# Three weighted tiles summed by VectorE, folded once by TensorE behind the next slot's first tile

## The chip, the cores and the metric

The kernel runs on one core of a Trainium2 chip. The metric is the device time of one execution in microseconds (us), lower is better; a profiled execution gives the trace that is read here. The engines of the core that matter are TensorE (PE; its weight loads are listed as PEld), VectorE (DVE), ScalarE (ACT), GpSimd (POOL, which here issues gathers) and SyncE (SP, which here only issues DMAs).

## What is computed

The reference runs a batch of 16 images (32 channels, 64 by 64 pixels) through four residual blocks, each behind a group normalisation: a Winograd convolution, a deformable convolution, a small network of quantised convolutions, and a convolution with an edge branch and channel attention. The change lies in the second block:

```python
py = hs[None, None, :, None] + ky[None, :, None, None] + dy
px = ws[None, None, None, :] + kx[None, :, None, None] + dx
sampled = _bilinear_sample(x, py, px)          # [B, C, 9 taps, H, W]
s = sampled.reshape(B, GROUPS, cin_g, KK, H, W)
wg = w.reshape(GROUPS, cout_g, cin_g, KK)
y = jnp.einsum('bgikhw,goik->bgohw', s, wg).reshape(B, Cout, H, W)
```

## The kernel before

**Images and slots.** The four blocks of three neighbouring images are interleaved. One image's work is a period of 24 slots (SLOTS), each of three steps q = 0, 1, 2. In period n every engine walks through the same slots: the deformable sampling of image n, then what stands in `c(n - 1, s, q)` (the last two blocks of the image before), `a(n + 1, s, q)` (the first block, the offsets and the tables of the next image) and `first(n + 2, s, q)`. Each engine's program is this list in order, written out by hand, with semaphores between the engines; an engine that waits holds up all that stands behind it. The periods 1 to 14 are one loop, which all engines leave and enter at its edge. A place is written (slot, step) below, as in the code.

**Two ways of sampling.** Of the nine taps, six (GTAPS) are gathered from a table in DRAM by GpSimd's indirect DMAs into `ring`, eight blocks deep, and VectorE weights the four corners of each sample (`weigh_corners`, line 1165), adds rows (`add_rows`, 1169) and adds columns (`add_columns`, 1175, which also frees the ring's block). The other three taps (DT) are sampled densely. A slot is one dense tap of one eighth of the image (a part; parts are g = s // 3, and e = s % 3 is the tap).

**A slot's dense work.** ScalarE makes `select`. TensorE makes three row tiles (`row_tile`, line 1445: three matmuls in the program, six in the trace, 128x512 out) into one of two banks of `ps_r`; tile t may start when tile t-2 has been weighed (`tile_weighed`). VectorE multiplies each with the hats of its columns (`weigh_tile`, line 1154), into `col_hat` itself, which is double buffered by slot and loaded by a DMA of SyncE (`load_cols`, line 460). At the end of a slot, behind its third tile and whatever stands at step 2, TensorE folds each of the three weighed tiles with four small matmuls (`fold_dense`, line 1457; 24 records a slot in the trace) into `ps_y`. In a part's last slot (e = 2) it also turns the gathered values (`turn`, line 1471) and folds them (`fold`, 1478), and ScalarE saves `ps_y` at the start of the next part (`save_conv`, 669).

**SyncE.** In a slot SyncE first issues the load of the next slot's `col_hat`, which waits until the slot before has been folded, and then the copies of the other blocks: `copy_taps` (line 410, twelve DMAs) behind the normalised images "norm1" (VectorE's place (12, 0)), "norm2" (3, 0) and "norm3" (19, 0), and `store_plane` and `load_taps` (416, 422) behind each "relu" (6, 1), (9, 2) and (12, 2). These bring the convolutions at TensorE's places (5, 2), (8, 2), (11, 2), (14, 1), (14, 2) and (21, 2) their input.

**Corner weights.** The weights of the gathered taps are computed for the next image at (22, 2) into `w_next` (line 1135), and copied to `w_cur` at (23, 0) (line 1210).

## Time and profile before

| | us |
|---|---|
| median of 3 runs | 4684.99 (4672.83 to 4689.32) |
| the profiled execution | 4687.73 |
| its span | 4685.9 |
| TensorE busy | 4264.4 (91%) |
| GpSimd busy | 3263.5 (70%) |
| VectorE busy | 2932.8 (63%) |
| ScalarE busy | 1812.5 (39%) |
| mean granted TensorE clock | 0.973 |

The busy time of an engine is the union of its instructions' times. It is an average over stages that have different limits: the same engine can have every microsecond taken in some slots and stand idle for 10 us in others. So the trace is also read by stretches of one period. A mean duration of an instruction is longer than the distance from its start to the next one's where instructions overlap in an engine's pipeline, which holds for TensorE above all.

### The profile page before, as it was taken

The numbers are of one execution on the slowest core, as the hardware profiler recorded it, in microseconds if no ns is written. First come the engines' busy times: TensorE is split into PE (matmuls) and PEld (weight loads), VectorE is DVE, ScalarE is ACT, GpSimd is POOL, SyncE is SP. The second block draws the span as 40 slices with busy tenths as digits, with TensorE's granted clock in tenths as the row PEclk, the third lists the DMA queues.
The fourth block names the chain that finished last, engine by engine and source line by source line (L and its number), as shares of the span: only waits on it lengthen the run. The fifth ranks groups of instructions, "written<-read, shape, count | busy, mean of one in ns | idle before, by whom it ended". The sixth has DMA issues, their size and how long they took to land.

```text
span 4685.9 us, 74289 instructions
## 1 busy us (share of the span) xinstructions
PE 4264.4 (91%) x24997; PEld 2037.6 (43%) x24997; DVE 2932.8 (63%) x5482; ACT 1812.5 (39%) x1991; POOL 3263.5 (70%) x3094
## 2 busy tenths in 40 slices
PE   2799999999999999999999999999999999999992
PEld 2344444444444444444444444444444444444440
DVE  4556666666656766666666656665666666656552
ACT  1343434344434433434344334434434344334331
POOL 1777777777777767777676777767777676767740
PEclk8899999999999999999999999999999999999995
DMA  4577877877878686777768777686777868778752
GB/s 104 197 232 214 240 232 221 236 223 227 235 222 240 208 245 215 231 235 224 237 215 240 222 222 230 212 244 209 237 230 220 237 214 243 219 218 244 219 185 66
DMA packets 479569, 1024.32 MB, mean 219 GB/s; under 512 B 261924, under 2 KB 298116, under 8 KB 474628
## 3 DMA queue, kind: packets, MB, share of 16 engines
q1 hardware_dynamic: 325636, 516.15, 38.7%
q10 hardware_dynamic: 55296, 302.01, 18.6%
q0 software_dynamic: 98304, 201.52, 15.5%
q8 instruction: 233, 3.82, 0.3%
q14 instruction: 100, 0.82, 0.1%
HBM read 864.66 MB, written 73.99 MB: 200 GB/s over the span
## 4 chain that ended last, share of the span: by engine, by line
PE 57%; DVE 16%; DMA 11%; SPq 9%; issue 6%; ACT 1%; ACTq 0%; POOL 0%; DVEq 0%; POOLq 0%
PE ps_r L1445 40%; SPq L410 6%; DMA col_hat<-coord_table 5%; PE ps_c L1431 4%; DVE col_hat L1154 4%; PE ps_y L1457 4%; DMA wino<-xn_a 3%; PE ps_a L1384 2%; DVE ring L1165 2%; PE ps_a L1431 2%; DMA taps_c<-plane_act 2%; PE ps_t L1471 1%; DVE ring L1169 1%; DVE values L1175 1%; PE ps_y L1478 1%
## 5 line engine op out<-in xcount | busy, mean ns | idle before, releaser
L593 POOL DMA_INDIRECT ring<-patch_table,idx_part x3072 | 3254.9, 1060 | 1258.8 <-issue 1049.5
L1445 PE MATMUL ps_r<-select,image 128*128 128x512 f32 x6912 | 3166.2, 606 | 73.9 <-issue 47.7
L1445 PEld LDWEIGHTS ps_r<-select,image 128*128 128x128 f32 x6912 | 1273.7, 192 | 1526.1 <-issue 1490.2
L1154 DVE TENSOR_TENSOR col_hat<-ps_r,col_hat 128x512 f32<-128x512 f32 x1152 | 793.4, 689 | 1530.1 <-PE ps_r L1445 1201.1
L643 ACT ACTIVATE select<-row_in,minus_row 128x1536 f32<-128x1536 f32 x384 | 605.0, 1575 | 765.3 <-PE ps_r L1445 698.5
L645 ACT ACTIVATE select<-select,one_col 128x1536 f32<-128x1536 f32 x384 | 605.3, 1576 | 12.5
L1165 DVE TENSOR_TENSOR ring<-ring,w_cur 128x768 f32<-128x768 f32 x512 | 487.2, 952 | 15.2 <-DMA ring<-patch_table,idx_part 13.2
L662 ACT COPY samples<-ps_t 128x512 f32<-128x512 f32 x256 | 149.6, 585 | 886.7 <-PE ps_t L1471 886.7
L1457 PE MATMUL ps_y<-col_hat,w_dense 128*32 128x128 f32 x9216 | 379.4, 279 | 100.8 <-DVE col_hat L1154 94.9
L1457 PEld LDWEIGHTS ps_y<-col_hat,w_dense 128*32 128x32 f32 x9216 | 215.8, 109 | 307.5 <-DVE col_hat L1154 160.7
L1169 DVE TENSOR_TENSOR ring<-ring 128x384 f32<-128x384 f32 x512 | 283.2, 553 | 4.4
L1175 DVE TENSOR_TENSOR values<-ring 128x192 f32<-128x192 f32 x512 | 181.6, 355 | 20.0
L1471 PEld LDWEIGHTS ps_t<-ident,values 128*128 128x128 f32 x1024 | 128.1, 141 | 135.6 <-issue 135.6
L1384 PEld LDWEIGHTS ps_a<-wino,w_freq 128*128 128x128 f32 x1152 | 141.9, 201 | 48.2 <-issue 26.1
L1384 PE MATMUL ps_a<-wino,w_freq 128*128 128x64 f32 x1152 | 142.5, 284 | 22.0 <-DVE wino L937 22.0
L1471 PE MATMUL ps_t<-ident,values 128*128 128x128 f32 x1024 | 153.9, 273 | 0.0
L669 ACT ACTIVATE conv_out<-ps_y,vec 128x128 f32<-128x128 f32 x128 | 46.7, 365 | 276.1 <-PE ps_y L1478 276.1
L710 ACT ACTIVATE work_c<-ps_c,bn_bias,bn_scale 128x512 f32<-128x512 f32 x160 | 116.7, 779 | 75.8 <-PE ps_c L1431 60.8
L678 ACT COPY wino<-ps_a 128x384 f32<-128x384 f32 x96 | 44.5, 479 | 251.5 <-PE ps_a L1384 245.1
L1431 PE MATMUL ps_a<-wino,w_off 96*32 96x512 f32 x768 | 96.4, 656 | 31.6 <-DMA wino<-xn_a 31.6
L1431 PE MATMUL ps_c<-taps_c,w_signs 96*32 96x512 bf16 x1152 | 75.7, 399 | 46.6 <-DMA taps_c<-plane_act 46.6
L1431 PE MATMUL ps_c<-taps_c,w_edge_conv 96*32 96x512 f32 x768 | 96.1, 636 | 12.4 <-DMA taps_c<-xn_c 12.4
(231 smaller groups left out, 2362.5 us busy)
## 6 DMA issues: line engine op xcount, KB each, us to landing
row_in<-coord_table ACTq DMA_DIRECT2D x384, 768.0 KB
col_hat<-coord_table SPq DMA_DIRECT2D x384, 768.0 KB
ring<-patch_table,idx_part POOLq DMA_INDIRECT x3072
taps_c<-plane_act SPq DMA_DIRECT2D x144, 268.1 KB
taps_c<-xn_c SPq DMA_DIRECT2D x192, 130.0 KB
coord_table<-wino SPq DMA_DIRECT2D x64, 216.0 KB
wino<-xn_a SPq DMA_DIRECT2D x96, 130.0 KB
plane_act<-act_c SPq DMA_DIRECT2D x192, 65.0 KB
```

The costliest lines, as they stand in the source:

```text
L410: sp.dma_start(dst[dx * C:(dx + 1) * C, lo - dx:hi - dx], src[s * C:(s + 1) * C, lo - s * RS * XW:hi - s * RS * XW]).then_inc(done, 16)
L593: nc.gpsimd.indirect_dma_start(out=ring[j][:, h % 2, k, :], out_offset=None, in_=table, in_offset=bass.IndirectOffsetOnAxis(ap=idx_part[:, ...
L643: nc.scalar.activation(sel, row_in[s % 2][:], ACT.Abs, bias=minus_row[:]).then_inc(row_in_read, 1)
L645: nc.scalar.activation(sel, sel, ACT.Relu, bias=one_col[:], scale=-1.0).then_inc(select_made, 1)
L1154: v.tensor_tensor(hat_t, ps_r[:, (s + t) % 2], hat_t, ALU.mult).then_inc(tile_weighed, 1)
L1165: return chain.add(v.tensor_tensor(tile, tile, wts, ALU.mult))
L1169: return chain.add(v.tensor_tensor(tile[:, :, 0:2 * C], tile[:, :, 0:2 * C], tile[:, :, 2 * C:], ALU.add))
L1384: ins = mm(ps_a[:, f % 2, b_ * NT:(b_ + 1) * NT], flat_w(w_freq, f * FREQ + b_), wino_v[:, f, :, b_, :], start=True, stop=True)
L1431: ins = mm(ps[s * C:(s + 1) * C, h], w[:, k0 + dy], src[:, r0:r0 + RS // 2, 0:W], start=(dy == 0), stop=(last and dy == 2))
L1445: ins = mm(ps_r[:, (s + t) % 2], image[:, m, t], select[s % 2][:, m], start=(m == 0), stop=(m == PAIRS - 1))
L1457: ins = mm(ps_y[j * C:(j + 1) * C, :], w_dense[:, DT - 1 - e].rearrange("p g o -> p (g o)"), col_hat[s % 2][:, t, j * P:(j + 1) * P], star ...
L1471: ins = nc.tensor.transpose(ps_t[:, j * P:(j + 1) * P], values[:, g % 2, j, 4 * k:4 * k + 4].rearrange("p k c -> p (k c)"), ident[:])
```

## The change

VectorE adds the three weighed tiles of a slot in two instructions (`sum_tiles`): tile 0 + tile 1 at step 1, and + tile 2 at step 2, both behind the gathered block's work of the step and ahead of the other blocks' work. The sum goes to a new double-buffered `tile_sum`. TensorE folds this sum alone, with four matmuls instead of twelve in the program, and does so one slot later, behind the next slot's first row tile (`fold_before`); the folds of the gathered values move with it. SyncE's load of `col_hat` now waits for the sums and no longer for the fold. ScalarE saves `ps_y` behind the next slot's `select` and no longer ahead of it. Two pieces of the other blocks swap their steps on VectorE in slot 0: `add_conv` goes from (0, 1) to (0, 2), and the first piece of `a` from (0, 2) to (0, 1). The corner weights are computed in place in `w_cur`, without the copy. The padded taps of `values` are gone: the second chunk of the turn reads taps 2 to 5 instead of 4 to 7, with zero weights for the two that the first chunk has had.

```diff
@@ SyncE, load_cols
                 if not known_zero(n) or s >= 2:
-                    sp.wait_ge(dense_folded, (n * SLOTS + s - 1) * WT)
+                    sp.wait_ge(tiles_summed, n * SLOTS + s - 1)
@@ ScalarE, slot
-                if e == 0 and live(before[0]):
-                    save_conv(*before)
                 if s != SLOTS - 2:
                     rows_ahead(n, s)
...
                 if e == 0 and live(n) and g < PARTS - 2:
                     place(n, g + 2)
+                if e == 0 and live(before[0]):
+                    save_conv(*before)
@@ VectorE, a and c
-                if at == (0, 2):
+                if at == (0, 1):
                     dve.wait_ge(halo_a, n * 32 + 32)
...
-                if at == (0, 1):
+                if at == (0, 2):
                     add_conv(n)
@@ VectorE, the corner weights at (22, 2)
+                    if not known_zero(n):
+                        dve.wait_ge(weighted, n * Q + RING)
...
-                        ins = v.tensor_tensor(w_next[:, :, :, i], hat[:, i // 2, 0, :, 0:GTAPS],
+                        ins = v.tensor_tensor(w_cur[:, :, :, i], hat[:, i // 2, 0, :, 0:GTAPS],
@@ VectorE, gathered_block
                             dve.wait_ge(a_dve.sem, a_dve.at(m, "weights"))
-                            if live(n):
-                                dve.wait_ge(weighted, m * Q + RING)
-                            chain.step(v.tensor_copy(w_cur[:], w_next[:]))
@@ VectorE, new
+            def sum_tiles(n, s, t):
+
+                to, hats = tile_sum[:, s % 2], col_hat[s % 2]
+                dve.wait_ge(tile_weighed, (n * SLOTS + s) * WT + t + 1)
+                if t == 1:
+                    if not known_zero(n) or s >= 2:
+                        dve.wait_ge(dense_folded, n * SLOTS + s - 1)
+                    tiles_added[0] = chain.add(v.tensor_tensor(to, hats[:, 0], hats[:, 1], ALU.add))
+                else:
+                    chain.upto(tiles_added[0])
+                    v.tensor_tensor(to, to, hats[:, 2], ALU.add).then_inc(tiles_summed, 1)
@@ VectorE, slot
                     gathered_block(n, s, q)
+                    if q > 0 and live(n):
+                        sum_tiles(n, s, q)
@@ TensorE, fold_dense
-                for t in range(WT):
-                    pe.wait_ge(tile_weighed, (n * SLOTS + s) * WT + t + 1)
-                    for j in range(JB):
-                        ins = mm(ps_y[j * C:(j + 1) * C, :],
-                                 w_dense[:, DT - 1 - e].rearrange("p g o -> p (g o)"),
-                                 col_hat[s % 2][:, t, j * P:(j + 1) * P], start=(e == 0 and t == 0), stop=False)
-                    ins.then_inc(dense_folded, 1)
+                pe.wait_ge(tiles_summed, n * SLOTS + s + 1)
+                for j in range(JB):
+                    ins = mm(ps_y[j * C:(j + 1) * C, :],
+                             w_dense[:, DT - 1 - e].rearrange("p g o -> p (g o)"),
+                             tile_sum[:, s % 2, j * P:(j + 1) * P], start=(e == 0), stop=False)
+                ins.then_inc(dense_folded, 1)
@@ TensorE, slot
                     if live(n):
                         row_tile(n, s, q)
+                    if q == 0:
+                        fold_before(n, s)
+                    if live(n):
                         if e == DT - 1 and q != 1:
                             turn(n, g, q // 2)
...
-                if live(n):
-                    fold_dense(n, s)
-                    if e == DT - 1:
-                        for k in range(CHUNKS):
-                            fold(n, g, k)
```

On TensorE, before, the first slot of the loop and the start of the second, with what each instruction waits for:

```order
414 L1445 MATMUL ps_r<-select,image 128x512 [waits tile_weighed]
415 L1445 MATMUL ps_r<-select,image 128x512 x2
417 L1445 MATMUL ps_r<-select,image 128x512 [waits tile_weighed,image_ready]
418 L1445 MATMUL ps_r<-select,image 128x512 x2
421 L1445 MATMUL ps_r<-select,image 128x512 [waits tile_weighed]
422 L1445 MATMUL ps_r<-select,image 128x512 x2
424 L1457 MATMUL ps_y<-col_hat,w_dense 32x128 [waits tile_weighed,conv_saved]
425 L1457 MATMUL ps_y<-col_hat,w_dense 32x128 x3
427 L1457 MATMUL ps_y<-col_hat,w_dense 32x128 [waits tile_weighed]
428 L1457 MATMUL ps_y<-col_hat,w_dense 32x128 x3
430 L1457 MATMUL ps_y<-col_hat,w_dense 32x128 [waits tile_weighed]
431 L1457 MATMUL ps_y<-col_hat,w_dense 32x128 x3
```

The same place in the changed kernel:

```order
312 L1469 MATMUL ps_r<-select,image 128x512 [waits tile_weighed]
313 L1469 MATMUL ps_r<-select,image 128x512 x2
315 L1480 MATMUL ps_y<-tile_sum,w_dense 32x128 [waits tiles_summed]
316 L1480 MATMUL ps_y<-tile_sum,w_dense 32x128 x3
318 L1501 MATMUL ps_y<-samples,w_dconv 32x128 [waits copied]
319 L1501 MATMUL ps_y<-samples,w_dconv 32x128 x3
321 L1501 MATMUL ps_y<-samples,w_dconv 32x128 [waits copied]
322 L1501 MATMUL ps_y<-samples,w_dconv 32x128 x3
324 L1469 MATMUL ps_r<-select,image 128x512 [waits tile_weighed,image_ready]
325 L1469 MATMUL ps_r<-select,image 128x512 x2
328 L1469 MATMUL ps_r<-select,image 128x512 [waits tile_weighed]
329 L1469 MATMUL ps_r<-select,image 128x512 x2
```

The three folds that waited for the slot's own weighed tiles are gone from its end. Behind the first tile stands one fold, of the slot before, and here, at a part's start, the folds of the gathered values too.

On VectorE, before, the second slot of the loop up to its third weighed tile:

```order
475 L1154 TENSOR_TENSOR col_hat<-ps_r,col_hat 128x512 [waits rows_made]
476 L1169 TENSOR_TENSOR ring<-ring 128x6x64 [waits dve_chain]
477 L893 BN_STATS bn_c<-x 128x6 [waits x2_ready]
478 L893 BN_STATS bn_c<-x 128x6
479 L895 BN_AGGR mv_c<-bn_c 128x2 [waits dve_chain]
481 L1154 TENSOR_TENSOR col_hat<-ps_r,col_hat 128x512 [waits rows_made]
482 L1175 TENSOR_TENSOR values<-ring 128x192 [waits turned,dve_chain]
483 L922 TENSOR_TENSOR wino<-xn_a 128x288
484 L923 SCALAR_TENSOR_TENSOR wino<-xn_a 128x288
485 L924 SCALAR_TENSOR_TENSOR wino<-xn_a 128x288
487 L1154 TENSOR_TENSOR col_hat<-ps_r,col_hat 128x512 [waits rows_made]
488 L1327 COPY x_cur<-x_next 128x1024 [waits x2_ready]
```

The same place in the changed kernel, from the second tile on:

```order
529 L1165 TENSOR_TENSOR col_hat<-ps_r,col_hat 128x512 [waits rows_made]
530 L1200 TENSOR_TENSOR values<-ring 128x192 [waits turned,dve_chain]
531 L1174 TENSOR_TENSOR tile_sum<-col_hat 128x512 [waits dense_folded,tile_weighed]
532 L930 TENSOR_TENSOR wino<-xn_a 128x288
533 L931 SCALAR_TENSOR_TENSOR wino<-xn_a 128x288
534 L932 SCALAR_TENSOR_TENSOR wino<-xn_a 128x288
536 L1165 TENSOR_TENSOR col_hat<-ps_r,col_hat 128x512 [waits rows_made]
537 L1177 TENSOR_TENSOR tile_sum<-tile_sum,col_hat 128x512 [waits dve_chain,tile_weighed]
538 L1351 COPY x_cur<-x_next 128x1024 [waits x2_ready]
```

Each of the two adds stands between the weighing of a tile and the other blocks' instructions, so all of these, and the weighing of the next tile, stand behind it.

## Rows read from the trace of the kernel before

**Rows 1.** The profile's page: busy times, and the chain that ended last by engine.

```profile
PE 4264.4 (91%) x24997; PEld 2037.6 (43%) x24997; DVE 2932.8 (63%) x5482; ACT 1812.5 (39%) x1991; POOL 3263.5 (70%) x3094
...
PE 57%; DVE 16%; DMA 11%; SPq 9%; issue 6%; ACT 1%; ACTq 0%; POOL 0%; DVEq 0%; POOLq 0%
```

**Rows 2.** Groups by line: busy us, mean ns, idle before them and its releasers.

```profile
L593 POOL DMA_INDIRECT ring<-patch_table,idx_part x3072 | 3254.9, 1060 | 1258.8 <-issue 1049.5 <-ACT idx_part L621 143.4 <-DVE values L1175 65.8
L1445 PE MATMUL ps_r<-select,image 128*128 128x512 f32 x6912 | 3166.2, 606 | 73.9 <-issue 47.7 <-DVE col_hat L1154 15.2 <-ACT image L654 10.8
...
L1154 DVE TENSOR_TENSOR col_hat<-ps_r,col_hat 128x512 f32<-128x512 f32 x1152 | 793.4, 689 | 1530.1 <-PE ps_r L1445 1201.1 <-DMA col_hat<-coord_table 325.2 <-issue 0.8
...
L1165 DVE TENSOR_TENSOR ring<-ring,w_cur 128x768 f32<-128x768 f32 x512 | 487.2, 952 | 15.2 <-DMA ring<-patch_table,idx_part 13.2
L1457 PE MATMUL ps_y<-col_hat,w_dense 128*32 128x128 f32 x9216 | 379.4, 279 | 100.8 <-DVE col_hat L1154 94.9 <-issue 2.3
L1169 DVE TENSOR_TENSOR ring<-ring 128x384 f32<-128x384 f32 x512 | 283.2, 553 | 4.4
...
L1210 DVE COPY w_cur<-w_next 128x768 f32<-128x768 f32 x16 | 10.3, 644 | 0.0
```

**Rows 3.** One period in nine windows: length, busy time by engine, clock, DMA share, GB/s.

```profile
2353.60:2382.60 29.00, 28.43 (x155) 13.56 (x154) 24.44 (x46) 11.11 (x11) 22.91 (x21) 1.00 0.48 171
2382.60:2405.90 23.30, 22.72 (x118) 11.81 (x116) 14.18 (x27) 9.17 (x9) 17.81 (x19) 1.00 1.01 294
2405.90:2444.20 38.30, 37.89 (x244) 19.58 (x243) 20.96 (x34) 14.79 (x17) 26.58 (x28) 1.00 0.60 185
2444.20:2466.40 22.20, 20.43 (x133) 9.74 (x132) 20.82 (x36) 11.76 (x14) 17.02 (x16) 1.00 0.57 195
2466.40:2489.50 23.10, 21.10 (x138) 10.25 (x137) 11.66 (x23) 6.81 (x9) 17.99 (x17) 1.00 0.79 222
2489.50:2516.60 27.10, 24.34 (x130) 10.06 (x132) 13.50 (x22) 9.52 (x8) 20.88 (x20) 1.00 0.98 259
2516.60:2578.50 61.90, 60.48 (x384) 29.36 (x377) 42.90 (x86) 27.05 (x31) 37.63 (x37) 1.00 0.82 240
2578.50:2606.70 28.20, 26.98 (x165) 11.57 (x164) 19.11 (x43) 9.23 (x12) 22.50 (x19) 1.00 0.79 211
2606.70:2632.90 26.20, 21.99 (x115) 10.27 (x115) 14.65 (x25) 13.34 (x16) 20.32 (x20) 0.87 0.91 287
```

**Rows 4.** TensorE's timeline at four places: start, duration, instructions, idle before them.

```profile
2324.36 0.86 PE L1457 MATMUL ps_y<-col_hat,w_dense 128*32 128x128 f32 x24
2325.15 5.42 PE L1445 MATMUL ps_r<-select,image 128*128 128x512 f32 x12
...
2344.36 0.62 PE L1478 MATMUL ps_y<-samples,w_dconv 128*32 128x128 f32 x16
2349.04 5.37 PE L1445 MATMUL ps_r<-select,image 128*128 128x512 f32 x8 [4.06 <-issue]
...
2505.38 0.42 PE L1457 MATMUL ps_y<-col_hat,w_dense 128*32 128x128 f32 x8 [0.21 <-issue]
2505.73 2.84 PE L1445 MATMUL ps_r<-select,image 128*128 128x512 f32 x6
```

**Rows 5.** Timelines of SyncE and VectorE around norm2, and of TensorE's waits for copies.

```profile
2385.36 8.71 SPq L410 DMA_DIRECT2D taps_c<-xn_c  x12
...
2405.86 0.69 DVE L1154 TENSOR_TENSOR col_hat<-ps_r,col_hat 128x512 f32<-128x512 f32 x1 [7.93 <-DMA col_hat<-coord_table]
...
2465.51 0.70 DVE L1224 TENSOR_SCALAR act_c<-work_c 128x1024 bf16<-128x1024 f32 x1
...
2484.06 1.50 PE L1431 MATMUL ps_c<-taps_c,w_signs 96*32 96x512 bf16 x24 [1.20 <-DMA taps_c<-plane_act]
...
2513.05 5.36 PE L1431 MATMUL ps_a<-wino,w_off 96*32 96x512 f32 x48 [1.46 <-DMA wino<-xn_a]
```

**Rows 6.** GpSimd's gathers by line while VectorE stood idle, 2398 to 2405.8 us.

```profile
L593 POOL DMA_INDIRECT ring<-patch_table,idx_part x7 | 6.6, 945 | 2.1 <-issue 2.1
```

29 lines of the change are left out of this document (22 added, 7 removed).

## The prediction

> **What bounds the kernel now.** I read the page first, then the groups by line, then one period cut into windows, then the timelines where a window shows an engine waiting. By its busy share TensorE is the bound: 4264.4 of 4685.9 us, against 2932.8 of VectorE [rows 1]. But the chain that ended last is only 57% TensorE; 16% of it is VectorE, 20% are DMAs and SyncE's issues [rows 1]. So the bound changes hands within a period, and one number for the kernel will not do. The windows show where [rows 3]. In slots 5 to 7, and 14 to 19, TensorE is busy for 37.89 of 38.30 and 60.48 of 61.90 us, and VectorE for little more than half or two thirds: TensorE's time. In slots 8 and 9 VectorE is busy for 20.82 of 22.20 us and TensorE for 20.43: VectorE's time. In slots 0 to 2 both are near full (28.43 and 24.44 of 29.00). The rest hangs on copies. The load of `col_hat` for slot 5 stands on SyncE behind the twelve copies that norm2 starts: 8.71 us of issues from 2385.36 on, and the tile is weighed only at 2405.86, after VectorE had stood for 7.93 us, 20.5 us behind norm2 whatever TensorE does meanwhile [rows 5]. The convolution at (11, 2) waited 1.20 us for its copy, which starts with the relu that ends at 2466.2, and the one at (14, 1) waited 1.46 us for a copy behind norm1 [rows 5].
>
> A third engine is close. A gather takes 1060 ns [rows 2] and about 0.30 us of issue follows it (2.1 us behind 7) [rows 6], so the 192 gathers of an image take 192 x 1.36 = 261 us. The period that I cut is 279.3 us (the sum of the nine windows) [rows 3]. GpSimd can shorten its waits by 18 us a period, no more.
>
> **What TensorE saves.** Today 24 small matmuls take 0.79 us from their start to the next tile's (2324.36 to 2325.15); 8 take 0.35 us (2505.38 to 2505.73) [rows 4]. That is 0.44 us a slot, 384 x 0.44 = 169 us. Ahead of the folds TensorE also waits for VectorE's last tile, 94.9 us in all [rows 2], 0.25 us a slot; behind the next slot's first tile (2.6 to 2.8 us) that wait is covered, if VectorE gets its weighing, a block's 0.95 and 0.55 us and the add done in this time. Together 264 us, 16.5 us a period, were TensorE the bound throughout.
>
> **What VectorE pays.** No instruction of before adds 128x512 from SBUF to SBUF. The 128x384 add takes 553 ns and the 128x768 product 952 ns [rows 2], so 128x512 lies between: 553 + 128 x (952 - 553) / 384 = 686 ns, and the weighing itself, of the same shape, takes 689 [rows 2]. Back to back such instructions overlap by some 0.04 us; I take 0.65 us of path for each, with 0.55 and 0.69 as the ends. Two a slot are 1.3 us, 31 us a period. The copy to `w_cur` that goes gives back 0.64 us a period [rows 2], in slot 23, where VectorE waits anyway: nothing. The waits of the adds for their own engine's results find them done, but for the drain. VectorE's busy time a period goes from 182 (the sum in rows 3) to 182 + 31 = 213 us: still under TensorE's, but not in every window.
>
> **By windows** [rows 3], change against before:
> - Slots 0 to 2. VectorE 24.44 + 3.9 = 28.3, and 0.5 us a slot that it idles even where it is the bound (slots 8 and 9: (22.20 - 20.82) / 2 = 0.7): 29.8 for 29.0, **+0.8**. TensorE's saving is lost here.
> - Slots 3 and 4. Norm2 to the weighing of slot 5 is a chain of issues and a DMA: **0**. The adds behind norm2 lie in VectorE's 7.93 us of idle time; without that cover they would cost 2.6.
> - Slots 5 to 7: three times 0.44 and some of the wait, **-1.5**.
> - Slots 8 to 11. VectorE 20.82 + 2.6 + 1.0 = 24.4 for 22.2 in the first two, +2.2, and with that the relu at the end of (9, 2), whose copy the convolution at (11, 2) awaits. In this period all of it would come through; TensorE's waits for such DMAs are not in all periods, so I take half, +1.1, and -0.5 for slot 11 behind the convolution: **+0.6**.
> - Slots 12 and 13. Norm1 stands ahead of the adds of its slot, the copies take what they take: **0**.
> - Slots 14 to 19. Six slots, 42.90 + 7.8 = 50.7 us of VectorE in 61.9: TensorE's. Six times 0.44 and part of 0.25: **-3.0**.
> - Slots 20 and 21. VectorE's edge values at (21, 2), which TensorE awaits, come behind one or two adds more, +1.3; the folds behind them are gone, -0.9: **+0.4**.
> - Slots 22 and 23: -0.5, and at the period's end 24 + 16 small matmuls (0.79 and 0.62 us less overlap) leave the path to the loop's edge, whose 4.06 us of issue stay [rows 4]; they return as 0.35 + 0.5 behind the first tile, in VectorE's time: -1.5. **-2.0**.
>
> The sum is -4.7 us a period, -66 over the 14 full ones; images 0 and 15, with only a part of the other blocks beside them, are more TensorE's, -8 each. -82 against 4687.7 of the profiled execution; against the median of the runs, 2.7 us lower, 4603.
>
> **What costs nothing.** ScalarE saves `ps_y` some 3 us later; the next writer is a fold a slot later, and ScalarE is busy for 39% [rows 1]. `add_conv` moved back by a step covers it. SyncE's `col_hat` load waits for sums: by about 1.5 us later where a block's product and add stand ahead, and several us earlier where TensorE had a convolution ahead of its folds. The turn reads other taps at the same size.
>
> **GpSimd, a bound on the gain.** A gather takes 945 ns while VectorE is idle [rows 6] and 1060 in the mean [rows 2]: 3072 x 0.115 = 353 us come with VectorE's work. Spread over all its 2932.8 us, the new 527 us of adds (768 x 0.686) cost 63 us; laid to the two large gather-side instructions alone (487.2 + 283.2 us [rows 2]), 242 us. That is 4 to 15 us a period, and I take 8, nearer to the mean of all: a floor of 261 + 8 = 269, at most 276. The forecast, 274.6, lies above the floor that I take and leaves GpSimd little. The Trainium skill (SBUF — State Buffer, "Who interferes with whom") says that a VectorE instruction with two SBUF inputs contends with a GpSimd instruction that reads SBUF, and that the loser is blocked fully; both adds are of that kind. By that rule the fifth case below would come; by the rows at most half of it is seen.
>
> **The rivals.**
> 1. The above, 4560 to 4660, likeliest 4603: 0.52.
> 2. TensorE is the bound nearly everywhere, since two banks of `ps_r` absorb VectorE's peaks. Then 16.5 us a period would go, but the gathers stop it at 269: -10 us a period, 4685 - 160 = 4525 (4490 to 4560). For it: TensorE's 95% in rows 3. Against: slots 8 and 9, and the fixed copies. 0.18.
> 3. VectorE's peaks eat the rest: another 4.7 us a period, no change, 4685 (4671 to 4699): 0.12.
> 4. VectorE becomes the bound: in slots 0 to 3, 8, 9, 12, 15, 17, 20 and 21 each slot costs the whole 1.3 us, +14.3, and the others give back 13 x 0.6 = 7.8: +6.5 a period, 4685 + 104 = 4789; half of it, 4740, is as likely. It decides from where a chain of slots has VectorE's busy time above about 95% of the length, as slots 0 to 2 (28.3 of 29) and 8 and 9 would. 0.13.
> 5. An add stops the gathers for as long as it runs: 527 us x GpSimd's 70% [rows 1] = 369 us, 23 us a period, 261 + 23 = 284 against 279.3: +4.9, 4763. Against it: the present VectorE instructions on `ring` alone would then cost 770 x 0.70 = 539 us, and all of the excess is 353. 0.05.
>
> **How the numbers follow.** 0.3% (14 us) is about what a measurement of this kernel can tell from no change. Case 1 lies wholly below it, and so does case 2: faster 0.70; case 3: same 0.12; cases 4 and 5: slower 0.18. The range leaves out the lower part of case 2 and the upper of 4 and 5, a tenth on either side: 4520 to 4710; case 1 alone has 4560 to 4660.
>
> **What would show it.** TensorE's fold group at 3072 records and a third of its busy time, and its wait for VectorE there near nothing; two groups of adds of 384 each at 0.68 us; the same windows: slots 14 to 19 shorter by 3 us, 8 and 9 longer by 2, 0 to 2 not shorter; the gathers' mean at 1.08 to 1.12 us. Wrong would be: a wait of VectorE for gathered blocks of more than some 50 us, or TensorE waiting at the row tiles for weighed tiles by more than 5 us a period (15.2 us in all for its matmuls [rows 2] today).

## The result, and the profile after

The changed kernel takes 4642.12 us (median of 4 runs, 4634.15 to 4647.02), the kernel before 4682.93 in the same comparison: ratio 0.9912, interval 0.9892 to 0.9933. A second comparison, on another chip (changed_again, below), gave 0.9862, interval 0.9843 to 0.9881. So it is faster by 0.9 to 1.4%. The forecast was 4603, faster by 1.7%: right in its sign and inside its range, too large in its size. The profiled execution's span went from 4685.9 to 4632.3 us, 53.6 less.

The profile's page after, busy times and the chain that ended last by engine, answers to [rows 1]:

```profile
PE 4106.7 (89%) x18853; PEld 1861.5 (40%) x18853; DVE 3381.6 (73%) x6236; ACT 1809.9 (39%) x1991; POOL 3343.7 (72%) x3094
...
PE 48%; DVE 23%; issue 10%; DMA 9%; SPq 7%; POOL 3%; ACT 0%; DVEq 0%; ACTq 0%; POOLq 0%
```

TensorE is busy for 157.7 us less, but the span is only 53.6 shorter: TensorE now idles for 104 us more than before (span less busy: 421.5 before, 525.6 now). Its part in the chain fell from 57 to 48%, VectorE's rose from 16 to 23.

The groups by line of the changed kernel, answering to [rows 2]:

```profile
L599 POOL DMA_INDIRECT ring<-patch_table,idx_part x3072 | 3335.5, 1086 | 1137.6 <-issue 1059.9 <-DVE values L1200 58.4 <-ACT idx_part L627 19.3
L1469 PE MATMUL ps_r<-select,image 128*128 128x512 f32 x6912 | 3201.2, 609 | 107.2 <-DVE col_hat L1165 57.9 <-ACT image L660 47.8 <-issue 1.5
...
L1190 DVE TENSOR_TENSOR ring<-ring,w_cur 128x768 f32<-128x768 f32 x512 | 486.7, 951 | 27.1 <-DMA ring<-patch_table,idx_part 27.1
...
L1177 DVE TENSOR_TENSOR tile_sum<-tile_sum,col_hat 128x512 f32<-128x512 f32 x384 | 265.1, 690 | 4.4
L1174 DVE TENSOR_TENSOR tile_sum<-col_hat 128x512 f32<-128x512 f32 x384 | 263.0, 685 | 0.0
...
L1480 PE MATMUL ps_y<-tile_sum,w_dense 128*32 128x128 f32 x3072 | 164.5, 286 | 148.7 <-DVE tile_sum L1177 147.1
```

The reader sees the books of the change. The fold's matmuls: 379.4 to 164.5 us busy, -215. Its wait for VectorE did not vanish, it grew: 94.9 to 147.1. The row tiles, whose 6912 matmuls nobody touched, are busy for 35 us more (3166.2 to 3201.2) and idle for 33 us more (73.9 to 107.2). The forecast had put the fold's group at a third of its busy time; it is 43%.

The same nine places of one period in the changed kernel, answering to [rows 3]:

```profile
2341.70:2371.40 29.70, 27.80 (x123) 12.50 (x113) 27.79 (x52) 11.66 (x11) 23.91 (x20) 1.00 0.52 180
2371.40:2392.80 21.40, 20.45 (x83) 10.46 (x82) 16.48 (x31) 8.89 (x10) 16.83 (x16) 1.00 1.00 299
2392.80:2430.40 37.60, 37.60 (x201) 18.86 (x200) 24.88 (x41) 14.80 (x17) 29.06 (x29) 1.00 0.60 189
2430.40:2454.20 23.80, 20.53 (x101) 9.04 (x100) 23.12 (x41) 11.86 (x14) 18.32 (x19) 1.00 0.62 213
...
2500.60:2559.40 58.80, 55.84 (x266) 25.90 (x266) 49.87 (x98) 26.20 (x31) 39.90 (x38) 1.00 0.81 244
2559.40:2591.70 32.30, 27.87 (x139) 11.06 (x140) 21.44 (x48) 8.95 (x13) 25.59 (x23) 0.95 0.80 226
2591.70:2616.20 24.50, 21.50 (x92) 9.31 (x86) 16.19 (x28) 14.43 (x16) 19.02 (x19) 0.93 0.79 246
```

In slots 8 and 9 (the fourth row) VectorE is now busy for 23.12 of 23.80 us; in slots 20 and 21 (the row before the last) TensorE is busy for 27.87 of 32.30, where it was 26.98 of 28.20. In the mean of twelve periods slots 8 and 9 take 1.6 us more (22.2 to 23.8; the forecast said 2), and slots 10 and 11 take 1.8 less.

One period is not the mean. The next table is worked out from the trace: for each of the 12 periods 2 to 13 the time from a slot's first weighing to that of the next, averaged and summed by groups of slots. Some of the experiments stand in it too.

| mean us in slots | 0-2 | 3-4 | 5-7 | 8-11 | 12-13 | 14-19 | 20-21 | 22-23 | period |
|---|---|---|---|---|---|---|---|---|---|
| before | 29.0 | 23.4 | 38.5 | 43.6 | 27.1 | 62.5 | 29.7 | 26.0 | 279.8 |
| changed | 29.1 | 23.4 | 37.3 | 43.4 | 25.7 | 59.3 | 33.3 | 24.8 | 276.3 |
| forecast difference | +0.8 | 0 | -1.5 | +0.6 | 0 | -3.0 | +0.4 | -2.0 | -4.7 |
| measured difference | +0.1 | 0.0 | -1.2 | -0.2 | -1.4 | -3.2 | **+3.6** | -1.2 | -3.5 |
| weights_in_place | 29.3 | 23.6 | 38.4 | 43.0 | 27.7 | 62.3 | 30.0 | 26.0 | 280.3 |
| changed_again | 28.9 | 23.7 | 37.7 | 43.5 | 24.2 | 60.5 | 33.4 | 24.9 | 276.7 |
| adds_alone | 31.2 | 26.0 | 39.9 | 46.4 | 27.7 | 64.0 | 32.3 | 27.7 | 295.2 |
| fold_at_end | 40.4 | 24.3 | 43.6 | 54.2 | 23.9 | 79.9 | 33.9 | 30.9 | 331.1 |
| placement_alone | 28.1 | 24.9 | 37.9 | 43.2 | 24.6 | 60.4 | 31.0 | 25.2 | 275.4 |
| edges_first | 28.9 | 23.8 | 37.4 | 43.5 | 25.9 | 59.3 | 33.0 | 24.7 | 276.6 |
| copies_split | 29.2 | 20.0 | 39.1 | 43.6 | 25.7 | 59.6 | 31.6 | 24.8 | 273.6 |
| placement_split | 27.7 | 21.0 | 38.6 | 42.7 | 24.3 | 60.5 | 28.9 | 24.9 | 268.6 |
| placement_ahead | 28.1 | 19.5 | 40.0 | 42.1 | 17.9 | 69.3 | 27.9 | 25.1 | 269.9 |
| adds_ahead | 29.0 | 19.5 | 39.5 | 43.6 | 18.4 | 67.8 | 30.9 | 24.8 | 273.6 |

How much two executions of the same kernel differ shows in changed_again, which is the changed kernel once more: 1.5 us in slots 12 and 13 and 1.2 the other way in slots 14 to 19, at most 0.4 elsewhere. Slots 12 to 19 taken together are steady, 85.0 and 84.7 us, for 89.6 before. All groups but two came within 0.9 us of the forecast; slots 20 and 21 missed it by 3.2 (29.7 and 30.0 us in the two traces without the change, 33.3 and 33.4 in the two with it), and slots 12 and 13 by 1.4 the other way, which is no more than two executions differ by. The timelines of SyncE and of VectorE in slots 20 and 21 of the changed kernel (start, duration, instructions, idle before them):

```profile
2558.33 4.96 SPq L416 DMA_DIRECT2D taps_c<-xn_c  x6
2563.70 6.98 SPq L466 DMA_DIRECT2D col_hat<-coord_table  x2
...
2565.33 1.89 DVE L1118 TENSOR_SCALAR wino<-wino 96x128 f32<-96x128 f32 x12
2567.14 0.68 DVE L1165 TENSOR_TENSOR col_hat<-ps_r,col_hat 128x512 f32<-128x512 f32 x1
2567.75 0.94 DVE L1190 TENSOR_TENSOR ring<-ring,w_cur 128x768 f32<-128x768 f32 x1
2568.72 0.56 DVE L1194 TENSOR_TENSOR ring<-ring 128x384 f32<-128x384 f32 x1
2569.20 0.69 DVE L1177 TENSOR_TENSOR tile_sum<-tile_sum,col_hat 128x512 f32<-128x512 f32 x1
...
2573.19 0.69 DVE L1165 TENSOR_TENSOR col_hat<-ps_r,col_hat 128x512 f32<-128x512 f32 x1 [0.94 <-DMA col_hat<-coord_table]
```

TensorE's timeline of the changed kernel in the same stretch:

```profile
2565.98 2.74 PE L1469 MATMUL ps_r<-select,image 128*128 128x512 f32 x6
2569.94 0.43 PE L1480 MATMUL ps_y<-tile_sum,w_dense 128*32 128x128 f32 x8 [1.22 <-DVE tile_sum L1177]
...
2576.71 2.78 PE L1455 MATMUL ps_c<-taps_c,w_edge_conv 96*32 96x512 f32 x24
2582.45 1.12 PE L1540 MATMUL ps_c<-work_c,w_edge 128*128 128x512 f32 x2 [2.97 <-DVE work_c L1336]
2583.51 4.48 PE L1455 MATMUL ps_c<-taps_c,w_edge_conv 96*32 96x512 f32 x24
```

Three things stand in these rows. (1) The tile that should cover the wait for the sum, 2.74 us from 2565.98, does not: VectorE comes to its weighing only at 2567.14, from a block of 1.89 us, and then has 0.68 + 0.94 + 0.56 + 0.69 us to do; the fold waits for 1.22 us. (2) VectorE waits at 2573.19 for the `col_hat` load of slot 21, which stands behind norm3's copies on SyncE. (3) TensorE waits for 2.97 us for the edge values, and the next 24 matmuls take 4.48 us where the same 24 took 2.78 just before.

### The profile page after: what moved, and what is told of

The parts are those of the page before. It is cut to its first block, busy times and chain, and to the rows that moved or that the text cites. A ratio compares the mean times of both kernels' runs of the same rounds, so it can differ in the third digit from the quotient of the medians.

```text
span 4632.3 us, 62891 instructions
## 1 busy us (share of the span) xinstructions
PE 4106.7 (89%) x18853; PEld 1861.5 (40%) x18853; DVE 3381.6 (73%) x6236; ACT 1809.9 (39%) x1991; POOL 3343.7 (72%) x3094
## 3 DMA queue, kind: packets, MB, share of 16 engines
q1 hardware_dynamic: 325636, 516.15, 38.4%
q0 software_dynamic: 98304, 201.52, 16.2%
## 4 chain that ended last, share of the span: by engine, by line
PE 48%; DVE 23%; issue 10%; DMA 9%; SPq 7%; POOL 3%; ACT 0%; DVEq 0%; ACTq 0%; POOLq 0%
PE ps_r L1469 33%; DMA col_hat<-coord_table 7%; SPq L416 5%; DVE col_hat L1165 4%; PE ps_c L1455 4%; DVE ring L1190 3%; POOL ring L599 3%; PE ps_a L1408 2%; DVE tile_sum L1174 2%; DVE ring L1194 2%; PE ps_y L1480 2%; PE ps_t L1494 2%; DVE tile_sum L1177 1%; PE ps_a L1455 1%; PE ps_c L1540 1%
## 5 line engine op out<-in xcount | busy, mean ns | idle before, releaser
L599 POOL DMA_INDIRECT ring<-patch_table,idx_part x3072 | 3335.5, 1086 | 1137.6 <-issue 1059.9
L1469 PE MATMUL ps_r<-select,image 128*128 128x512 f32 x6912 | 3201.2, 609 | 107.2 <-DVE col_hat L1165 57.9
L1190 DVE TENSOR_TENSOR ring<-ring,w_cur 128x768 f32<-128x768 f32 x512 | 486.7, 951 | 27.1 <-DMA ring<-patch_table,idx_part 27.1
L1480 PE MATMUL ps_y<-tile_sum,w_dense 128*32 128x128 f32 x3072 | 164.5, 286 | 148.7 <-DVE tile_sum L1177 147.1
L1177 DVE TENSOR_TENSOR tile_sum<-tile_sum,col_hat 128x512 f32<-128x512 f32 x384 | 265.1, 690 | 4.4
L1174 DVE TENSOR_TENSOR tile_sum<-col_hat 128x512 f32<-128x512 f32 x384 | 263.0, 685 | 0.0
L1480 PEld LDWEIGHTS ps_y<-tile_sum,w_dense 128*32 128x32 f32 x3072 | 62.9, 108 | 451.6 <-issue 319.0
L1494 PEld LDWEIGHTS ps_t<-ident,values 128*128 128x128 f32 x1024 | 117.6, 141 | 95.7 <-issue 92.9
L748 ACT ACTIVATE work_c<-ps_c,bias 128x512 f32<-128x512 f32 x32 | 22.0, 687 | 250.8 <-PE ps_c L1540 250.8
```

Source lines behind the costliest of these rows:

```text
L599: nc.gpsimd.indirect_dma_start(out=ring[j][:, h % 2, k, :], out_offset=None, in_=table, in_offset=bass.IndirectOffsetOnAxis(ap=idx_part[:, ...
L1174: tiles_added[0] = chain.add(v.tensor_tensor(to, hats[:, 0], hats[:, 1], ALU.add))
L1190: return chain.add(v.tensor_tensor(tile, tile, wts, ALU.mult))
L1469: ins = mm(ps_r[:, (s + t) % 2], image[:, m, t], select[s % 2][:, m], start=(m == 0), stop=(m == PAIRS - 1))
L1480: ins = mm(ps_y[j * C:(j + 1) * C, :], w_dense[:, DT - 1 - e].rearrange("p g o -> p (g o)"), tile_sum[:, s % 2, j * P:(j + 1) * P], start= ...
L1494: ins = nc.tensor.transpose(ps_t[:, j * P:(j + 1) * P], values[:, g % 2, j, chunk_start(k):chunk_start(k) + 4].rearrange("p k c -> p (k c) ...
```

## The experiments

My theory after the result: the change is two changes. The move of the fold behind the next slot's first tile pays; the adds cost on VectorE what their matmuls save on TensorE, and more; and a fixed chain at norm3, overlooked in the forecast, takes back part of the gain. The rivals: that the sum is what pays, the place of the fold only serving it; that the price lies in the order on VectorE (a sum that comes too late behind a gathered block, edge values behind the adds) or in contention with the gathers, not in VectorE's total.

All runs are of 5 rounds; the ratios are against the kernel before in the same comparison. There were three comparisons, each on a chip of its own. The kernel before had a median of 4697.48 in that of weights_in_place, adds_alone, fold_at_end and edges_first, of 4709.05 in that of placement_alone, copies_split, sum_first and fold_later, and of 4703.88 in that of the last four kernels. The changed kernel itself ran only in the last of them; a kernel of the other two is set against its two ratios, 0.9912 and 0.9862, and a difference from it of less than these 0.5% can't be told.

### weights_in_place

The kernel before with the corner weights computed in place, `w_next` and the copy gone.

```diff
-                        ins = v.tensor_tensor(w_next[:, :, :, i], ...
+                        ins = v.tensor_tensor(w_cur[:, :, :, i], ...
-                            chain.step(v.tensor_copy(w_cur[:], w_next[:]))
```

> The kernel before with the corner weights computed in place and no copy to w_cur, nothing else. Both theories: ratio 1.000 to the kernel before. The copy takes 0.64 us once a period, in slot 23, where VectorE waits for TensorE for several us. If the copy were on the path after all, 10 us would go (0.998).

Measured: 4698.84 us, 1.0011 (0.9992 to 1.003). Nothing, as forecast.

### adds_alone

The kernel above, with the two adds at their places on VectorE; nothing reads the sum, TensorE folds three tiles at the slot's end as before. SyncE's load of `col_hat` waits for the sum besides the fold.

```diff
                     gathered_block(n, s, q)
+                    if q > 0 and live(n):
+                        sum_tiles(n, s, q)
```

> The kernel before (weights in place) with VectorE's two adds a slot, whose sum nothing reads; TensorE still folds three tiles at the slot's end. So this is the price of the adds with none of TensorE's gain. Theory A, VectorE's place in the chains (edge values at (21, 2), relu at (9, 2), slots 0 to 3) takes the gain back: about 1.3 us in each of the 6 to 8 slots that VectorE bounds, 6 to 10 us a period, 4780 to 4840, ratio 1.02 to 1.035. Theory B, the adds slow GpSimd's gathers and these set the period: gathers of 267 us and 7.5 us between images make 275, below the 280 of before, so the adds alone cost under 1 us a period: ratio 1.00 to 1.003.

Measured: 4909.18 us, 1.0448 (1.0416 to 1.0479); the period is 295.2, 15.4 more. That is above what either theory gave. Its groups by line:

```profile
L1459 PE MATMUL ps_r<-select,image 128*128 128x512 f32 x6912 | 3220.0, 614 | 97.8 <-issue 56.0 <-DVE col_hat L1158 38.9 <-ACT image L656 2.9
...
L1471 PE MATMUL ps_y<-col_hat,w_dense 128*32 128x128 f32 x9216 | 380.4, 279 | 223.2 <-DVE col_hat L1158 222.7 <-issue 0.4
```

With the fold in its old place the adds cost 212 us (4909.18 against 4697.48) for 528 us of work: TensorE's wait at the fold grows by 128 us (94.9 to 222.7), its row tiles by 54 busy and 24 idle.

### fold_at_end

The changed kernel, with its single fold put back at the slot's end, behind its own sum.

```diff
-                    if q == 0:
-                        fold_before(n, s)
...
+                if live(n):
+                    fold_dense(n, s)
```

> The changed kernel with its single fold back at the slot's end, where TensorE waits for the slot's own sum. Theory A: the wait for the last weighing, the block's product and add and the sum (1.4 to 2.9 us, less where a convolution stands ahead) is on TensorE's path in most slots, some 1 us a slot over the changed kernel, and the 0.44 us a slot of saved matmuls stays: ratio to the kernel before 1.02 to 1.05. Theory B: TensorE has that time to spare as long as the period stays above 275 us: ratio 0.99 to 1.00.

Measured: 5487.87 us, 1.1688 (1.1654 to 1.1722), far outside what either side expected. Its groups by line, and below them its TensorE timeline over two slots:

```profile
L1469 PE MATMUL ps_r<-select,image 128*128 128x512 f32 x6912 | 3436.1, 649 | 66.3 <-issue 65.1 <-ACT image L660 1.2
...
L1480 PE MATMUL ps_y<-tile_sum,w_dense 128*32 128x128 f32 x3072 | 180.3, 309 | 813.5 <-DVE tile_sum L1177 813.5
```

```profile
2596.35 7.99 PE L1469 MATMUL ps_r<-select,image 128*128 128x512 f32 x18
2608.32 0.43 PE L1480 MATMUL ps_y<-tile_sum,w_dense 128*32 128x128 f32 x8 [3.97 <-DVE tile_sum L1177]
2608.67 9.69 PE L1469 MATMUL ps_r<-select,image 128*128 128x512 f32 x18
```

In 337 of 384 slots TensorE now waits for VectorE to weigh its last tile, do the gathered block's work and add: 813.5 us, 719 more than before, 1.9 us a slot. And behind the wait the same 18 row matmuls take 9.69 us where they took 7.99: the row tiles are busy for 270 us more. 719 + 270 - 199 (the fold's matmuls) = 790, of a span that is 798 longer. So the sum does not pay at all without the move, and a wait costs more than its length.

### placement_alone

No adds: the fold of all three tiles is moved behind the next slot's first tile. A third `col_hat` buffer holds the tiles, and a load waits for the slot before to be weighed, where it waited for it to be folded. The weights in place and the other small parts of the change are in it. The cut is against the kernel before.

```diff
-                    sp.wait_ge(dense_folded, (n * SLOTS + s - 1) * WT)
+                    sp.wait_ge(tile_weighed, (n * SLOTS + s - 1) * WT)
+                if not known_zero(n) or s >= 3:
+                    sp.wait_ge(dense_folded, (n * SLOTS + s - 2) * WT)
...
+                    if q == 0:
+                        fold_before(n, s)
-                if live(n):
-                    fold_dense(n, s)
```

> No adds: TensorE folds the three weighed tiles with the twelve matmuls of before, but behind the next slot's first row tile as in the changed kernel (a third col_hat buffer keeps the loads at their old times). The weights in place, the later save_conv and the swapped pieces of slot 0 stay. Theory A2, the placement is what pays and the adds cost more than the saved matmuls give: TensorE's wait at the fold (94.9 us before) nearly goes and VectorE has no more work than before, so 4560 to 4640, ratio 0.975 to 0.99, at or below the changed kernel's 0.991. Theory B2, the saved matmuls are what pays: without them the ratio is 0.995 to 1.005.

Measured: 4609.2 us, 0.979 (0.9771 to 0.981), better than the whole change. What the third buffer, the load's other wait and the small parts are worth in it was not measured apart, but for the weights in place (nothing). VectorE's waits for `col_hat` loads did not get shorter by them: 347.4 us, 325.2 before. Its groups:

```profile
L1454 PE MATMUL ps_r<-select,image 128*128 128x512 f32 x6912 | 3199.5, 608 | 108.5 <-DVE col_hat L1166 60.7 <-ACT image L661 46.2 <-issue 1.5
...
L1466 PE MATMUL ps_y<-col_hat,w_dense 128*32 128x128 f32 x9216 | 332.3, 277 | 2.7 <-DVE col_hat L1166 2.7
```

Without adds the wait at the fold is covered indeed: 2.7 us for 94.9 before. With them it is 147.1. The matmuls that the sum saves at this place are 332.3 - 164.5 = 168 us; the waits it brings are 144 at the fold. The row tiles' 33 us more of busy time and 35 of idle time stand here too, without any add, so they came with the move and not with the sum.

### copies_split

The changed kernel, with the twelve copies behind norm2 and norm3 issued as six and six, the load of the next `col_hat` between them.

```diff
                     sp.wait_ge(c_dve.sem, c_dve.at(n, "norm2"))
-                    copy_taps(taps_c[:], xn_c, taps_c_in)
+                    copy_taps(taps_c[:], xn_c, taps_c_in, 0)
+                if s == 4:
+                    copy_taps(taps_c[:], xn_c, taps_c_in, 1)
```

> The changed kernel with the twelve copies behind norm2 and norm3 split on SyncE: six in slots 3 and 19, six in slots 4 and 20 behind that slot's col_hat load. Theory C, the chain norm to copies to col_hat to weighing (20.6 us behind norm2, 22.1 behind norm3) sets slots 3 and 4, 19 and 20: the load starts some 3 to 4 us earlier, VectorE's waits for col_hat (258.7 us in all) shrink by a third, 3 to 5 us a period go, ratio to the kernel before 0.975 to 0.982. Rival, the transfer and not the issue is what takes the time (11 to 12 us for 768 KB beside the copies' own traffic), or TensorE's own work fills these slots: 0.988 to 0.992.

Measured: 4596.88 us, 0.9768 (0.9747 to 0.9788); against the changed kernel's own two ratios that is 0.9 to 1.5% less. From the norm to the weighing that hangs on the load (mean of 12 periods) it is 17.2 us for 20.6 at norm2, and 19.5 for 22.1 at norm3. VectorE's group of weighings shows where the wait went:

```profile
L1171 DVE TENSOR_TENSOR col_hat<-ps_r,col_hat 128x512 f32<-128x512 f32 x1152 | 792.7, 688 | 953.3 <-PE ps_r L1475 743.6 <-DMA col_hat<-coord_table 152.6 <-issue 54.7
```

Idle time that a `col_hat` load ended: 152.6 us, 258.7 in the changed kernel, 325.2 before. The load is issued 5.7 us behind norm2 for 8.3, and 5.9 behind norm3 for 10.1. The chain through SyncE's queue is real, at both places. Slots 3 and 4 took 3.4 us less by it, slots 20 and 21 1.7 (slot 20 alone is back from 15.6 us to 12.9), and slots 5 to 7 gave 1.8 of that back.

### edges_first

The changed kernel, with each add of slot 21 put behind the other blocks' work of its step. VectorE computes the edge values in two instructions, at (21, 1) and (21, 2). The first add moves behind the one at (21, 1) and still stands ahead of the one at (21, 2), so that only the second add leaves their path.

```diff
-                    if q > 0 and live(n):
+                    if q > 0 and live(n) and s != 21:
                         sum_tiles(n, s, q)
...
+                    if q > 0 and live(n) and s == 21:
+                        sum_tiles(n, s, q)
```

> The changed kernel with the two sums of slot 21 behind the other blocks' work of their steps, so that the edge values that TensorE awaits at (21, 2) come 1.3 us earlier. Nothing else moves. Theory A: TensorE's wait of 3.0 us there goes back to about 1.5, the clock isn't halved behind it (3.4 us at half speed in slot 21 of ten periods), so 1.3 to 3 us a period go: 4595 to 4622, ratio to the kernel before 0.981 to 0.987. Theory B: no change against the changed kernel, 0.991.

Measured: 4628.69 us, 0.9866 (0.9837 to 0.9896), between the changed kernel's two ratios, so no difference can be told. The edge values end 8.8 us behind the slot's first weighing, in the mean of 12 periods, 9.3 in the changed kernel; it is 0.4 to 0.5 us that the run took back and not the 1.3 expected. TensorE's wait for them did not fall with it (35.1 us in all, 33.6 in the changed kernel), and slots 20 and 21 took 33.0 us for 33.3.

So this run does not clear the adds. The kernels without adds show their part: there the edge values end 8.1 to 8.2 us behind the first weighing, as in the kernel before (8.1), so the two adds cost 1.1 us on that path. TensorE's wait for them is 14.8 us in placement_alone, and in the pair that differs in the sum alone it is 16.2 (placement_ahead) and 36.4 (adds_ahead).

### sum_first

The changed kernel, with each add ahead of the gathered block's work in place of behind it.

```diff
-                    gathered_block(n, s, q)
                     if q > 0 and live(n):
                         sum_tiles(n, s, q)
+                    gathered_block(n, s, q)
```

> The changed kernel with each add right behind the weighing and ahead of the gathered block's work. The sum is ready 0.95 to 1.5 us earlier at two of three slots' ends; VectorE's total work is the same but for a drain (0.1 us an add). Theory D, TensorE's wait at the fold (147.1 us in 123 waits) and the half clock that follows a wait are where the gain went: the wait falls to about 70 us, the row tiles' busy time from 3201 back to about 3180, ratio 0.975 to 0.984. Rival, VectorE's total work sets these slots whatever its order: 0.989 to 0.995.

Measured: 4683.77 us, 0.9943 (0.9924 to 0.9962): slower than the changed kernel by 0.3 to 0.8% (0.9912 and 0.9862), and in no case faster. Its groups:

```profile
L1469 PE MATMUL ps_r<-select,image 128*128 128x512 f32 x6912 | 3235.7, 612 | 143.5 <-DVE col_hat L1165 95.3 <-ACT image L660 45.4 <-issue 1.5
...
L1480 PE MATMUL ps_y<-tile_sum,w_dense 128*32 128x128 f32 x3072 | 164.9, 286 | 80.4 <-DVE tile_sum L1177 80.2
```

The wait at the fold fell from 147.1 to 80.2, as it should, and the time got longer: the row tiles' wait for weighed tiles rose from 57.9 to 95.3 and their busy time by 35. An earlier sum alone is no cure: what the fold gains by it the row tiles lose.

### fold_later

The changed kernel, with the fold behind the next slot's second tile.

```diff
-                    if q == 0:
+                    if q == (1 if s > 0 else 0):
                         fold_before(n, s)
```

> The changed kernel with the fold one row tile later still, behind the next slot's second row tile (behind the first in slot 0). Theory D: TensorE then has 5.4 us of row tiles between its slot's last tile and the fold, the wait at the fold goes to under 30 us; where VectorE is behind, part of it comes back at the row tiles (57.9 us there now): ratio 0.974 to 0.984. Rival, VectorE's total work sets these slots: the wait moves to the row tiles whole, 0.989 to 0.995.

Measured: 4706.18 us, 0.9993 (0.9974 to 1.0011): the whole gain is gone, more than either side expected. Its groups:

```profile
L1469 PE MATMUL ps_r<-select,image 128*128 128x512 f32 x6912 | 3246.8, 615 | 207.5 <-DVE col_hat L1165 151.9 <-ACT image L660 53.3 <-issue 1.7
...
L1480 PE MATMUL ps_y<-tile_sum,w_dense 128*32 128x128 f32 x3072 | 164.3, 286 | 5.3 <-DVE tile_sum L1177 5.3
```

The fold waits for 5.3 us now, and the row tiles for 151.9 us in place of 57.9. These two waits together are 157 us here, 176 in sum_first, 205 in the changed kernel, and 63 in placement_alone: the wait can be moved about; with adds it never fell below the 110 us of the kernel before, without them it is 63 or less. Moving it to the row tiles was dearer, though the sum was smaller; why is not fully shown (the row tiles' busy time and VectorE's waits for loads, 319.3 for 258.7, both rose, and TensorE's granted clock stood at the lower of its two levels for 259 us, 164 in the changed kernel).

### changed_again, placement_split, placement_ahead, adds_ahead

The first is the changed kernel once more, as a control.

> The changed kernel itself once more, as the control of this group. All theories: 0.991 to the kernel before, within 0.989 to 0.993.

Measured: 4642.53 us, 0.9862 (0.9843 to 0.9881), a little below what was expected.

The second is placement_alone with the split copies of copies_split.

> No adds, three tiles folded behind the next slot's first row tile (placement_alone), together with the twelve copies of norm2 and norm3 split in two sixes (copies_split). If the two gains are apart (TensorE's wait at the fold; the chain of copies ahead of col_hat), they add: 0.979 x 0.986 = 0.965, 0.962 to 0.969. If both came out of the same slots: 0.974 to 0.979.

Measured: **4530.15 us, 0.9634** (0.9616 to 0.9653), the best of all, 3.7% below the kernel before. The chain that ended last, and the groups:

```profile
PE 73%; DVE 7%; DMA 7%; SPq 5%; issue 4%; POOL 3%; ACT 0%; ACTq 0%; DVEq 0%; POOLq 0%
```

```profile
L1460 PE MATMUL ps_r<-select,image 128*128 128x512 f32 x6912 | 3165.0, 603 | 55.3 <-ACT image L667 44.4 <-DVE col_hat L1172 9.4 <-issue 1.5
...
L1472 PE MATMUL ps_y<-col_hat,w_dense 128*32 128x128 f32 x9216 | 332.7, 277 | 1.2 <-DVE col_hat L1172 1.1
```

TensorE waits for weighed tiles for 9.4 + 1.1 us in all and is 73% of the chain. The split is worth 1.6% here (0.9634 / 0.979, two ratios of different comparisons).

The third is placement_alone with the `col_hat` loads issued two slots ahead, not one.

```diff
-                if not known_zero(n) or s >= 2:
-                    sp.wait_ge(tile_weighed, (n * SLOTS + s - 1) * WT)
...
-                if live(n + (s + 1) // SLOTS):
-                    load_cols(n + (s + 1) // SLOTS, (s + 1) % SLOTS)
+                if live(n + (s + 2) // SLOTS):
+                    load_cols(n + (s + 2) // SLOTS, (s + 2) % SLOTS)
```

> placement_alone with its third col_hat buffer used: each load is issued two slots ahead of its use, as soon as the slot three before is folded. No load then stands between a norm's copies and the next weighing. Chain theory: VectorE's waits for col_hat (347 us in placement_alone) all but go, slots 3 and 4 from 24.9 to about 20, 19 to 21 by 2 us, ratio 0.955 to 0.966. Rival, TensorE's convolutions await the same copies and take the stall over: 0.970 to 0.979.

Measured: 4536.12 us, 0.9649 (0.9628 to 0.9669). VectorE waits for no load any more, slots 12 and 13 took 17.9 us for 24.6, and slots 14 to 19 69.3 for 60.4: the time of slot 13 came back a few slots later.

The fourth is the third with the adds (into the slot's own first tile) and the single fold.

> placement_ahead with the changed kernel's two adds a slot (made in place in tile 0 of col_hat) and its single fold: the two kernels differ in nothing but adds against matmuls. If the adds cost more than the eight matmuls a slot give back also with the copies' chain gone, it is slower than placement_ahead by 5 to 12 us a period, ratio 0.972 to 0.995. If in the changed kernel only the chain of copies hid TensorE's gain, it is faster than placement_ahead by 3 to 6 us a period: 0.940 to 0.955.

Measured: 4597.81 us, 0.9776 (0.9758 to 0.9794). It differs from placement_ahead in the adds and in the folded tiles, and takes 1.4% more. The groups of placement_ahead:

```profile
L1452 PE MATMUL ps_r<-select,image 128*128 128x512 f32 x6912 | 3166.9, 604 | 49.8 <-ACT image L659 44.8 <-DVE col_hat L1164 3.6 <-issue 1.5
...
L1464 PE MATMUL ps_y<-col_hat,w_dense 128*32 128x128 f32 x9216 | 333.1, 277 | 3.7 <-DVE col_hat L1164 3.7
```

and those of adds_ahead:

```profile
L1466 PE MATMUL ps_r<-select,image 128*128 128x512 f32 x6912 | 3197.2, 608 | 52.8 <-ACT image L659 47.3 <-DVE col_hat L1164 4.0 <-issue 1.5
...
L1477 PE MATMUL ps_y<-col_hat,w_dense 128*32 128x128 f32 x3072 | 164.1, 285 | 146.8 <-DVE col_hat L1174 145.4
```

This is the sum by itself, with the chains of loads out of the way: -169 us of matmuls, +142 of waits for the sum, +30 on the row tiles. TensorE is busy for 111 us less (4221.0 to 4109.6) and idle for 171 more (311.1 to 482.1), so the span is 60 us longer (4532.1 to 4591.7).

## Why the prediction was right in sign and 39 us too low

**Right.** The adds at 685 and 690 ns (forecast 686). The matmuls saved: 169 us forecast, 332.3 - 164.5 = 168 at equal place, 379.4 - 164.5 = 215 with the effect of the place on their records. The gathers at 1086 ns, inside 1.08 to 1.12 us, which is 80 us in all or 5 a period (8 taken, 4 and 15 as ends); VectorE's waits for gathered blocks are 27.1 us, 13.2 before, well under the 50 named as a sign of being wrong. So rival 5 did not come. Rival 2 (4490 to 4560) did not either. At equal place the adds lengthened the gathers by 106 us (3247.2 to 3352.8, placement_ahead and adds_ahead) or 84 (3251.5 to 3335.5, placement_alone and the changed kernel). That is a quarter of the 369 of rival 5; what the kernel before showed of it, 353 of 539, was two thirds and not "at most half". The Trainium skill (SBUF — State Buffer, "Who interferes with whom") has the shared ports as an exclusive lock, which would stop the gathers for as long as an add runs. It also infers there that a `tensor_tensor` takes the read side only and the making of descriptors needs the write side, by which they would not meet. The 84 to 106 us of 528 lie between the two. Slots 0 to 2, 3 and 4, 5 to 7 and 14 to 19 came within 0.7 us. The copy to `w_cur` cost nothing (weights_in_place).

**The step that failed: slots 20 and 21, forecast +0.4, measured +3.6.** I had read the chain norm2, twelve copies on SyncE, `col_hat` load, weighing as a fixed length [rows 5], and not asked whether norm3 starts one too. It does: from norm3's end to the weighing of slot 21 took 20.6 us before, the same as at norm2, with 1.24 us of idle VectorE at its end (mean of 12 periods); it takes 22.1 now, with 2.74 (21.7 and 2.4 in changed_again). What slots 14 to 19 save ahead of it can't shorten it, so part of it comes back: slot 19's length fell by 1.4 us, and that of slot 20, where VectorE waits for the load, grew by 3.0, from 12.6 to 15.6. The other 1.5 us is the chain's own growth. The load is issued 10.1 us behind norm3, as before (10.2), so it is the load and not the queue that takes longer; why is open. Where the load is issued between the copies, slot 20 takes 12.9 us, and without the adds as well (placement_split) slots 20 and 21 take 28.9, less than before.

Slot 21 is longer by 0.7 us, and there the forecast's own terms held: the adds put the edge values back by 1.1 us (1.3 forecast), and TensorE's wait for them rose from 19.5 to 33.6 us in all. With the loads out of the way the adds raise it too (16.2 to 36.4, placement_ahead and adds_ahead), so it belongs to the adds and not to the chain.

The 3.2 us a period that this step missed are 45 us over 14 periods. The spans missed the forecast by 28 (-53.6 for -82), as slots 12 to 19 gave 4.6 us a period where 3.0 were forecast, while image 0 gave 0.5 of its 8.

**"That wait is covered": right for the place, wrong for the sum.** The forecast had a condition, that VectorE gets a weighing, a block and an add done within one tile. It held without the add (2.7 us of wait) and did not with it (147.1): VectorE comes late to the last weighing from its other blocks. At the place shown, weighing, block and add take 2.75 us (2567.14 to 2569.89), as long as the tile that is to cover them (2.74), so that each bit of lateness becomes a wait, of 1.22 us there. I had taken VectorE's busy time in a window for its limit; what counts is how far it lies behind when TensorE reaches the fold.

**What the sum left out: the clock.** The same row matmuls are busy for 35 us more (33 of it already in placement_alone, and the sum brings 30 in the pair with the loads out of the way). Between the first and the last weighing TensorE's granted clock stood at the lower of its levels for 106 us before and for 164 in the changed kernel (133 in placement_alone, 61 in placement_split, 79 in placement_ahead and 154 in adds_ahead; changed_again has 177). It sits behind TensorE's waits, as in the rows of slot 21: each of the 24 stretches before and of the 34 now begins in or close behind a wait of 1.7 us or more.

The books of the whole: the fold's matmuls -215, its idle time +48, the row tiles +35 busy and +33 idle, the wait for the edge values +14, other busy time +22, other idle time +9; together -54.

**Right by luck.** The price of the adds was put wholly into windows where VectorE is in the way (+0.8, +0.6, +1.3 in slots 20 and 21) and the gain to both parts together. The experiments part them: the move, with the third buffer and the small parts, is worth -2.1%, the sum +0.7 to +1.4% on top of it (0.9912 and 0.9862 against 0.979; 1.4% in the pair made for it). The forecast did not say that one half of the change would be better alone.

**Open.** What sets slots 12 and 13, which the forecast left alone, is a third chain of the same form. In the kernel before:

```profile
2492.30 8.20 SPq L410 DMA_DIRECT2D wino<-xn_a  x12
2500.61 1.93 SPq L416 DMA_DIRECT2D plane_act<-act_c  x4
2502.84 0.67 SPq L460 DMA_DIRECT2D col_hat<-coord_table  x1
...
2516.57 0.69 DVE L1154 TENSOR_TENSOR col_hat<-ps_r,col_hat 128x512 f32<-128x512 f32 x1 [11.25 <-DMA col_hat<-coord_table]
```

The load of slot 14 stands behind norm1's twelve copies and the four stores behind the relu, and VectorE is idle for 11.2 us for it (mean of 12 periods; 8.4 in the changed kernel, 6.9 in changed_again), longer than at norm2 (8.0). With the loads two slots ahead it is gone, and slots 12 and 13 are shorter (24.6 to 17.9 us), but over slots 12 to 19 that brought nothing (85.0 us in placement_alone, 87.2 in placement_ahead). What this chain costs is open; no run split these copies. Images 0 and 1 gained nothing (252.4 to 251.9 and 283.6 to 285.4 us; forecast -8 for image 0), image 15 some 10, of which 6 is what two traces without the change differ by (247.0 and 241.4). How the price of the adds divides between VectorE's lateness, the gathers and the clock is only bounded by the groups above. Loads two slots ahead together with split copies were not tried, nor the parts of placement_alone one by one.

## What to carry to other kernels

Work moved from the busiest engine to one with room costs nothing only if that engine isn't the one that the busiest then waits for: look how late its queue is where the result is needed, not at its busy share. Try the parts of a change apart, for a move that is meant to serve the other half may be all of the gain. See that an edit takes all of the suspect out of the path, or a run without effect says little. And when a chain of fixed length (copies on a queue ahead of a load) is found at one place, look for every other place with the same form before anything upstream of it is credited with a gain.
